# Attention of a four-stage transformer chain: context in groups of four units, kept as columns, with a new order of work on every engine

## The reference, cut to what matters

```python
scores = jnp.einsum('bhqd,bhkd->bhqk', q / math.sqrt(HEAD_DIM), k)
scores = scores + attention_bias
scores = jnp.where(src_mask, -jnp.inf, scores.astype(jnp.float32))
probs = jax.nn.softmax(scores, axis=-1).astype(v.dtype)
ctx = jnp.einsum('bhqk,bhkd->bhqd', probs, v)
ctx = ctx.transpose(0, 2, 1, 3).reshape(B, S, D)
x = x + (ctx @ Wo + bo)
```

## Time and profile before

| what | value |
|---|---|
| median of 3 runs | 3475.27 us (3473.83 to 3478.54) |
| profiled execution, its own time | 3475.8 us |
| span of that profile | 3474.0 us |
| PE busy | 3408.8 us (98%) |
| DVE, ACT, POOL busy | 2343.6, 2278.9, 2395.8 us |
| attention block | about 490 to 2492 us of the span |
| granted TensorE clock, mean | 0.992 |

### The profile page before, as it was taken

How to read it: one execution, slowest core, us unless ns; L and a number is a source line. 1 busy time by engine, 2 the same in 40 slices (tenths; PEclk the granted TensorE clock), 3 DMA queues, 4 the chain that set the end, 5 groups by cost and what they waited for, 6 DMA issues and landing times. The chain is left out here.

```text
span 3474.0 us, 84659 instructions
## 1 busy us (share of the span) xinstructions
PE 3408.8 (98%) x33299; PEld 2692.7 (78%) x33299; DVE 2343.6 (67%) x5039; ACT 2278.9 (66%) x3399; POOL 2395.8 (69%) x942
## 2 busy tenths in 40 slices
PE   7999989999999999999999999999999999999998
PEld 3444448888888888888888888888778888887886
DVE  7776758888888888888888888888623232332333
ACT  2433449999999999999999999999622212221321
POOL 1222249999999999999999999999643324232322
PEclk8999999999999999999999999999999999999998
DMA  6666599888898988898888998888644544564463
GB/s 215 225 235 239 197 367 349 325 337 331 333 401 329 338 331 333 341 389 337 332 332 329 367 370 334 331 327 329 246 144 154 167 137 157 164 191 143 154 210 124
DMA packets 342721, 954.80 MB, mean 275 GB/s; under 512 B 33204, under 2 KB 190004, under 8 KB 267576
## 3 DMA queue, kind: packets, MB, share of 16 engines
q1 hardware_dynamic: 337108, 940.95, 73.4%
q10 hardware_dynamic: 5220, 8.42, 0.6%
HBM read 849.63 MB, written 99.62 MB: 273 GB/s over the span
## 5 line engine op out<-in xcount | busy, mean ns | idle before, releaser
L1249 POOL TENSOR_TENSOR at_tiles<-at_tiles,at_negmask 128x1920 f32<-128x1920 f32 x509 | 1950.7, 3896 | 29.9 <-DMA at_tiles<-in_bias 19.0
L1349 ACT ACTIVATE at_tiles<-at_tiles,at_rmin 128x2048 f32<-128x2048 f32 x512 | 1030.5, 2013 | 2.4 <-DVE at_rmin L1409 2.4
L1288 PE MATMUL at_ps_p<-consts,at_tiles 128*128 128x128 f32 x8192 | 1023.6, 272 | 1.7 <-ACT at_prob_t L1359 1.3
L1288 PEld LDWEIGHTS at_ps_p<-consts,at_tiles 128*128 128x128 f32 x8192 | 936.3, 139 | 72.5 <-DVE at_prob_t L1420 2.0
L1359 ACT ACTIVATE at_prob_t<-at_ps_p 128x512 f32<-128x512 f32 x1664 | 898.2, 603 | 125.0 <-PE at_ps_p L1288 124.9
L1409 DVE CUSTOM_DVE_ANT_0 at_tiles<-at_ps_s,at_tiles,at_rmin 128x1024 f32<-128x1024 f32 x512 | 655.0, 1279 | 171.7 <-PE at_ps_s L1273 171.0
L1267 PE MATMUL at_ps_s<-at_k_stack,at_q_stack 128*128 128x512 f32 x2048 | 700.7, 438 | 8.1 <-DVE at_rmin L1409 6.1
L1409 DVE CUSTOM_DVE_ANT_0 at_tiles<-at_ps_s,at_tiles 128x1024 f32<-128x1024 f32 x512 | 623.9, 1219 | 24.5 <-POOL at_tiles L1249 22.2
L1307 PE MATMUL at_ps_c<-at_prob_t,at_v 128*32 128x128 f32 x16384 | 500.3, 274 | 1.0 <-DVE at_ctx_rows L1437 1.0
L1307 PEld LDWEIGHTS at_ps_c<-at_prob_t,at_v 128*32 128x32 f32 x16384 | 431.6, 110 | 44.2 <-issue 43.0
L1267 PEld LDWEIGHTS at_ps_s<-at_k_stack,at_q_stack 128*128 128x128 f32 x2048 | 310.8, 191 | 62.5 <-issue 51.5
(11 more groups left out here) (239 smaller groups left out, 4098.3 us busy)
## 6 DMA issues: line engine op xcount, KB each, us to landing
at_tiles<-in_bias SPq DMA_DIRECT2D x512, 1024.0 KB, 6.3
ff_w_card<-w_mix SPq DMA_DIRECT2D x256, 256.0 KB, 2.7
ff_w_card<-in_W SPq DMA_DIRECT2D x192, 256.0 KB, 2.9
at_k_stack<-k_hi SPq DMA_DIRECT2D x128, 256.0 KB, 5.6
at_k_stack<-k_lo SPq DMA_DIRECT2D x128, 256.0 KB, 5.6
negm<-em_mask_out SPq DMA_DIRECT2D x32, 512.0 KB, 6.5
at_q_stack<-q_hi SPq DMA_DIRECT2D x128, 128.0 KB, 5.3
at_q_stack<-q_lo SPq DMA_DIRECT2D x128, 128.0 KB, 5.3
```

The source lines that it names most:

```text
L1249: pool.tensor_tensor(tiles[s][:, 0:PCOLS], tiles[s][:, 0:PCOLS], negm[s][:, 0:PCOLS], ALU.add).then_inc(s_pool, 1)
L1288: last = pe.transpose(ps_p[k][:, y * P:(y + 1) * P], tiles[s][:, t * P:(t + 1) * P], ident)
L1349: act.activation(tiles[s][:, :], tiles[s][:, :], ACT.Exp, bias=rmin[:, s, 1:2], scale=-1.0, accum_out=rsum[:, s:s + 1]).then_inc(s_exp, 1)
```

## The change

- `pv(g)` now takes four units at once: the four column groups of the array hold four units, and each runs over all 16 blocks of keys. It has 128 matmul records for four units, and stands behind the transposes of the first unit of the next group. Its result is the context with features and units on the partitions and queries on the columns: nothing is added up and nothing is turned back.
- The reciprocals of the row sums are brought to the same form: `invert(g)` writes the reciprocal of four row sums, each repeated 32 times (128 x 128), `rinv_columns(g)` turns it on TensorE, `take_rinv(g)` copies it, and `context(g)` multiplies the result of `pv` with it in one instruction.
- The probabilities lie in five buffers of one unit each instead of two of two units.
- `pool_columns` goes from S - 128 to S - 192: POOL adds the mask to 1856 columns, TensorE to 192.
- The context goes to memory as columns, one store of 64 KB for each group (128 in all), issued by SP.
- `ffn_stage` loads them as columns, in 16 DMAs of 64 KB for each tile (`read_ctx`), and `out_project` reads them as they come. `ctx_columns` and `take_ctx` are gone. `row_bank` exchanges the first two banks of `out_project` in some tiles.
- The order of the work in a group of four is new on TensorE, ACT and DVE.

```diff
-    at.pool_columns = S - 128
+    at.pool_columns = S - 192
-    at.p_t = [sb(f"at_prob_t{i}", [P, 2, S // P, P]) for i in range(2)]
+    at.p_t = [sb(f"at_prob_t{i}", [P, S // P, P]) for i in range(4)]
+    at.p_t += [sb("at_prob_t4", [P, S // P, P])]
...
+            def store(g):
+                n, s, b, qh, h = place(4 * g)
+                sp.wait_ge(s_cxo, g + 1)
+                sp.dma_start(net.ctx[(b * QH + qh) * 2 + s // 4, h], cx_t[g % 2][:]).then_inc(s_st[g % 2], 16)
...
                         if s == 2:
                             load_v(n + 1)
+                        if s % 4 == 2:
+                            store(2 * n + s // 4 - 1)
...
-            def pv(pr):
+            def pv(g):
+                pe.wait_ge(s_rc, g + 1)
...
+                for u in range(4 * g, 4 * g + 4):
                     for c in range(CH):
                         k, i = bank(u, c)
                         pe.wait_ge(s_pe[k], i + 1)
-                for i in range(QUART):
-                    for g in range(4):
...
+                for t in range(KT):
+                    for j in range(4):
+                        last = pe.matmul(ps_c[j * HD:(j + 1) * HD, 0:P], v_sb[n % 2][:, t, :], p_t[(4 * g + j) % NPT][:, t, :],
+                                         start=(t == 0), stop=(t == KT - 1))
-            def parts_rows(pr):
+            def rinv_columns(g):
+                pe.wait_ge(s_rv, g + 1)
+                after(pe, s_cxo, g)
+                pe.transpose(ps_c[:, P:2 * P], rinv[:].rearrange("p j d -> p (j d)"), ident).then_inc(s_rt, 1)
+            for g in range(-4, NG + 2):
+                u = 4 * g
                 qk(u + 3, 1)
+                transposes(u, (1, 2))
                 qk(u + 4, 0)
+                transposes(u, (3,))
+                pv(g - 1)
+                transposes(u + 1, (0,))
                 qk(u + 4, 1)
+                transposes(u + 1, (1, 2))
                 qk(u + 5, 0)
                 transposes(u + 1, (3,))
                 transposes(u + 2, (0, 1))
                 qk(u + 5, 1)
+                transposes(u + 2, (2,))
                 qk(u + 6, 0)
+                rinv_columns(g)
+                transposes(u + 2, (3,))
+                transposes(u + 3, (0,))
                 qk(u + 6, 1)
+                transposes(u + 3, (1,))
                 qk(u + 7, 0)
+                transposes(u + 3, (2, 3))
+                transposes(u + 4, (0,))
...
(ACT)
+            for g in range(-4, NG + 2):
+                u = 4 * g
+                take(u + 1, 3); take(u + 2, 0); take(u + 2, 1); take(u + 2, 2)
+                exp(u + 4)
+                take(u + 3, 0); take(u + 3, 1); take(u + 3, 2); take(u + 3, 3)
+                exp(u + 5)
+                exp(u + 6)
+                take(u + 4, 1); take(u + 4, 2); take(u + 4, 3)
+                exp(u + 7)
+                take(u + 5, 1); take(u + 5, 2)
...
(DVE)
+            def invert(g):
+                s = 4 * g % RING
+                dve.wait_ge(s_exp, 4 * g + 4)
+                after(dve, s_rt, g)
+                v.reciprocal(rinv[:], rsum[:, s:s + 4].unsqueeze(2).broadcast_to([P, 4, HD])).then_inc(s_rv, 1)
+            def take_rinv(g):
+                dve.wait_ge(s_rt, g + 1)
+                v.tensor_copy(rinv_t[:], ps_c[:, P:2 * P]).then_inc(s_rc, 1)
+            def context(g):
+                dve.wait_ge(s_pv, g + 1)
+                dve.wait_ge(s_rc, g + 1)
+                after(dve, s_st[g % 2], 16 * (g // 2))
+                v.tensor_tensor(cx_t[g % 2][:], ps_c[:, 0:P], rinv_t[:], ALU.mult).then_inc(s_cxo, 1)
+            for g in range(-4, NG + 2):
+                u = 4 * g
+                scores(u + 12, 0); take(u + 9, 0); scores(u + 12, 1)
+                invert(g + 2); context(g + 1)
+                scores(u + 13, 0); scores(u + 13, 1); scores(u + 14, 0)
+                take(u + 10, 3)
+                scores(u + 14, 1); take_rinv(g + 2); scores(u + 15, 0)
+                take(u + 12, 0)
+                scores(u + 15, 1)
...
+        def read_ctx(sp, n):
+            blocks = net.ctx[n].rearrange("(c i) (u d) q -> i d c u q", i=P // HD, d=HD)
+            for i in range(P // HD):
+                to = net.cx[i * HD:(i + 1) * HD].rearrange("p c (u q) -> p c u q", q=P)
+                for c in range(DC):
+                    sp.dma_start(to[:, c], blocks[i][:, c]).then_inc(net.s_cx, 16)
...
-                        pe.wait_ge(s_ct_out, 4 * n + k + 1)
-                        last = pe.matmul(ps_m[j][:], t2[:, k, j * P:(j + 1) * P], wo[:, k, :],
+                        last = pe.matmul(ps_m[row_bank(n, j)][:], cx[:, k, j * P:(j + 1) * P], wo[:, k, :],
```

More of the change, by code:

```diff
@@ L1239, in _ @@
                             load_v(n + 1)
+                        if s % 4 == 2:
+                            store(2 * n + s // 4 - 1)
             load_ffn()
+            for g in range(NG - 3, NG):
+                store(g)
+            for i in range(2):
+                sp.wait_ge(s_st[i], 16 * NG // 2)
         @block.gpsimd
@@ L1388, in _ @@
                 take(u + 2, 1)
-                store(pr - 3)
-                store(pr - 2)
-            store(NP - 1)
-            for i in range(RING // 2):
-                act.wait_ge(s_st[i], 16 * B * QH)
+                take(u + 2, 2)
+                exp(u + 4)
+                take(u + 3, 0)
+                take(u + 3, 1)
+                take(u + 3, 2)
+                take(u + 3, 3)
+                exp(u + 5)
+                exp(u + 6)
+                take(u + 4, 1)
+                take(u + 4, 2)
+                take(u + 4, 3)
+                exp(u + 7)
+                take(u + 5, 1)
+                take(u + 5, 2)
         @block.vector
@@ L1416, in take @@
                 k, i = bank(u, c)
[L1417 to L1418 removed]
+                after(dve, s_pv, (u - NPT) // 4 + 1)
                 dve.wait_ge(s_pt[k], i + 1)
[L1420 removed]
+                v.tensor_copy(p_t[u % NPT][:, 4 * c:4 * c + 4, :].rearrange("p t q -> p (t q)"),
                               ps_p[k][:]).then_inc(s_pe[k], 1)
[L1423 to L1424 removed]
+            def invert(g):
+                if not 0 <= g < NG:
@@ L1433, in context @@
-                after(dve, s_st[s // 2], 16 * (n // HEADS))
-                dve.wait_ge(s_rv, 2 * pr + 2)
-                for j in range(2):
-                    own = slice(j * HD, (j + 1) * HD)
-                    v.scalar_tensor_tensor(cx_all[:, s + j, h * HD:(h + 1) * HD], ps_c[:, P + 2 * HD:2 * P][:, own],
-                                           rinv[:, j:j + 1], cx_sb[:, own], ALU.mult, ALU.add).then_inc(s_cxo, 1)
-            def parts(pr):
-                if not 0 <= pr < NP:
-                    return
-                dve.wait_ge(s_pv, pr + 1)
-                v.tensor_copy(cx_sb[:], ps_c[:, 0:P]).then_inc(s_cxs, 1)
@@ new lines, in _ @@
+            for g in range(-4, NG + 2):
+                u = 4 * g
+                scores(u + 12, 0)
+                take(u + 9, 0)
+                scores(u + 12, 1)
+                invert(g + 2)
+                context(g + 1)
+                scores(u + 13, 0)
+                scores(u + 13, 1)
+                scores(u + 14, 0)
+                take(u + 10, 3)
+                scores(u + 14, 1)
+                take_rinv(g + 2)
+                scores(u + 15, 0)
+                take(u + 12, 0)
+                scores(u + 15, 1)
@@ L2002, in _ @@
                     x3_columns(z)
-                else:
-                    ctx_columns(n)
                 up(p, 4, 1)
```

177 lines of the change are left out of this document (41 added, 136 removed).

## The result

The changed kernel takes 3505.94 us (median of 4 runs, 3502.67 to 3508.51) against 3475.01 before; the ratio is 1.0087, with a 95% interval of 1.0069 to 1.0104. The profiled execution has a span of 3503.7 us, 29.7 more than before. The forecast was 3407, the range 3382 to 3450.

What follows compares the result with a forecast made beforehand. TensorE was taken as the bound, POOL 0.1 us behind; a group's steps sum to 15.04 us, 15.11 with waits, against 15.50. Attention 50, FFN 16 and seam 2 us make 68 off 3475.8: 3407 us, range 3382 to 3450.

Steps and rivals of the forecast that it cites:

- the tight place: Behind `qk(u+5,1)`: DVE's chain of 6.35 us plus hand-over makes TensorE 0 to 0.25 us late; ACT's `take(u+3,1)` as close.
- rival 1: Attention: no gain from neighbours at each `qk`, or PE waits more for banks; group 15.25 to 15.45, total 3427 to 3453; chance 0.14.
- I take 0.29, since in two elements none of it shows.: DVE's 128 x 128 reciprocal in `invert`: taken at the lower bound 0.29 us; upper bound about 1.0 us.
- `pv` has 17 waits in one place: TensorE before `pv`: 17 waits instead of nine in each of two places; if not hidden, up to 0.09 us later.
- These waits overlap; I add 0.07 us.: TensorE's waits for DVE's and ACT's copies in a group: 0.07 us added to 15.04, giving 15.11 us.
- V "as before", 2 x 1.88.: The product `pv`, 128 records for four units: 3.76 us, as before.
- The mask: TensorE's mask product, 64 columns more in each unit: 0.11 us for four units.
- FFN: Behind the attention: without `ctx_columns` 12.6 us less over seven tiles, with the first tile's wait together 16 us.
- rival 4: FFN: 16 load issues plus late cards stop TensorE 2 us or more in a tile; 16 us gone, 3423; chance 0.07.
- Seam: From the last context to the FFN's first matmul: 2 us of gain, between -2 and +5.
- Rival 2: POOL or bias becomes the bound: 3440 us if the add doesn't shrink, 3420 to 3433 if biases come late; chance 0.10.
- Rival 3: Slow reciprocal, 1.0 us, moves DVE's tight chain later by 0.7 us: group 15.75 to 15.95, total 3490 to 3515; chance 0.07.

Runs made afterwards that it cites:

- the moved reciprocal: Changed kernel with the reciprocal moved into VectorE's idle stretch during V, a group later, its transpose behind V: 3475.27 us; with three waits as well, 3459.56 us.
- the three waits: Changed kernel with three waits in front of V instead of sixteen, only the last copy of each of three banks: 3465.65 us, ratio to before 0.9972.
- the shifted program: Kernel with twelve of the sixteen waits issued earlier, plus 256 fulfilled waits once ahead of the attention, shifting the program half a transfer: 3551.16 us.

## Why the prediction was wrong

It had a group at 15.11 us and the attention 50 us shorter; a group is 15.83 in the mean and the attention 46 us longer. The 0.72 us between them are, by the runs: 0.33 that the moved reciprocal and the three waits take away together (15.83 to 15.50), 0.18 irregular gaps that are left in that kernel, and 0.21 by which its regular group (15.32) is over the forecast. The other 7.6 us of the attention are the first V, 10.8 us later, less an end that is 3.2 us shorter; the later first V is in no step of the prediction.

The 15.32 can be followed against the 15.04 of the sum, by the medians of the steps: the tight place +0.30, the block and turn behind V +0.05, the four `qk` with the mask product +0.04, small ones +0.02, V itself -0.13. The other blocks ahead of a `qk` cost what the sum had (0.36, 0.79 and 1.23 us), so the first half of rival 1 did not occur; the tight place may be its second half.

- *"I take 0.29, since in two elements none of it shows."* This failed. Of two bounds, 0.29 and 1.0, the row chosen (two elements) could not tell them apart, as the prediction itself said of them, and it was read as evidence for one. Measured: 0.95. Moved out of the chain, it gives back 31 us; cut to 0.35 in place, 28. Only a small part of that is DVE's chain itself; the larger part of the 31 is the step into V, where the late queue had to pay for its waits.
- *"`pv` has 17 waits in one place ... starts later by up to the 0.09 us that its lead is now."* The place was right and the size was not. The lead without excess waits is the 0.53 us of the sum (0.53 measured); with the waits it is 0.83 and 0.72 in turn, up to 0.30 us more and not 0.09. Eight or nine instructions of 0.106 us stand there, and the queue reaches them only 0.14 us before the four transposes start. Three waits give back 40 us. This was a larger term than the reciprocal by itself, and most of either is contained in the other: with the reciprocal moved, the same sixteen waits cost 0.02 us of the regular group.
- *"These waits overlap; I add 0.07 us."* In the kernel freed of both, the tight place has 0.29 us (three steps above), partly offset by V at 3.63 us for 3.76. It lies at the chunks (u+3,1) to (u+4,0), the second of the two places that the prediction named, at about four times the size; at chunk (u+4,3) nothing is late. Which wait makes it stays open.
- *V "as before", 2 x 1.88.* True of its length when it runs through. That it can outrun the supply of its instructions was not among the steps or rivals. It is behind most of the irregular 0.15 to 0.18 us per group; the stops inside V are 0.08 to 0.09 of it.
- *The mask*: 0.04 us for 0.11 in the kernel before, 0.05 in the new order (15.32 less 15.27). *FFN*: 15 us for 16, and PE waits for no card, so rival 4 did not occur; the 16 issues for the first tile took 9.20 us and not 6.9, and one load of 64 KB landed 2.2 us after its issue in the median. *Seam*: 1.4 for 2.
- *Rival 2*: with 192 columns POOL takes 3.71 us to the next start, as the prediction had it, and waits for biases for 120.8 us in all. At 14.8 us for four it was no bound of a group of 15.83.
- *Rival 3*, slow reciprocal, had 3490 to 3515 us and a group of 15.75 to 15.95, and both came out. But its mechanism, DVE's chain later by 0.7 us, carries at most the 0.24 us by which the four transposes at that place are long; the waits in front of V, the tight place that was there anyway and the gaps supplied the rest. That its number came out was luck: a sum of causes most of which it did not name.

## What to carry to other kernels

Price an instruction whose two bounds are far apart at the bound that hurts when it is to stand in an engine's tight chain, and put it where the engine is idle anyway: here 3 us lay free shortly ahead of it. Count waits as instructions of TensorE's queue: two shared one instruction of 0.106 us here. They cost nothing while the queue is further ahead than they take (eight waits in the kernel before), and what they take beyond that is paid in full (up to 0.30 us for seventeen), so wait once on the last copy of a chain, and look for what keeps the queue from running ahead. A long block of narrow products may outrun the supply of its own program: compare mean and median of the period. Splitting the block where it starts at a bad place of a transfer took the stops away here, but no clear time.

## What the hardware showed unexpectedly

- Fulfilled waits go two to an instruction, one instruction each 0.106 us of TensorE's queue. Eight in front of V cost nothing, sixteen more 118.1 us in 256 places, 0.46 us each time.
- 128 records of V in 3.63 us can stop for up to 3.1 us (3.5 with the shifted program) with nothing waited for, and the clock was at its lower level after the longest stop. In blocks of 64 this is 1.2 us in the whole run instead of about 10. The stops end at one place of each 256 instructions, 1.2 to 1.6 us after a packet of 16 KB has landed.
- A copy of 128 x 128 from SBUF to SBUF took 1.81 us in the mean beside GpSimd's additions, from PSUM 0.285; it ended 0.084 us after the addition did. The reciprocal of the same shape, also from SBUF to SBUF, took a steady 0.95 beside them.
